# The loads of split q and k with the head dimension as outermost index

## What is computed

```python
# B = 16, N = 512, D = 128, H = 16 heads, hd = 8
qkv = x @ w_qkv + b_qkv
q, k, v = jnp.split(qkv, 3, axis=-1)             # each to (B, H, N, hd)
q = jax.nn.elu(q) + 1
k = jax.nn.elu(k) + 1
attn_num = jnp.einsum('bhid,bhjd->bhij', apply_rope(q), apply_rope(k))
attn_denom = jnp.einsum('bhid,bhjd->bhij', q, k)
out = jnp.einsum('bhij,bhjd->bhid', attn_num / attn_denom, v)
x = x + out.transpose(0, 2, 1, 3).reshape(B, N, D) @ w_out + b_out
```

## Time and profile before

| | us |
|---|---|
| median of 3 runs | 4204.29 (4202.71 to 4212.35) |
| the profiled execution, its own time | 4196.47 |
| its span, from the first to the last instruction | 4194.5 |
| PE busy | 3514.4 (84%) |
| ACT busy | 3228.1 (77%) |
| DVE busy | 2902.8 (69%) |
| POOL busy | 1500.8 (36%) |

### The profile page before, as it was taken

The page is one execution under the profiler, slowest core; times in us unless marked ns, Lnnn a source line. Parts: engine busy times, 40 slices in busy tenths (PEclk is TensorE's granted clock), DMA queues, the critical chain, the costliest instruction groups (busy, mean ns, idle before and its releaser), DMA issues.

```text
span 4194.5 us, 39166 instructions
## 1 busy us (share of the span) xinstructions
PE 3514.4 (84%) x11446; PEld 1492.4 (36%) x11446; DVE 2902.8 (69%) x3513; ACT 3228.1 (77%) x4037; POOL 1500.8 (36%) x758
## 2 busy tenths in 40 slices
PE   3877598988889898988889898898989888898857
PEld 1131243433333343333334333333334333333423
DVE  2426568768686767868686777858677786858592
ACT  2667588887888787888878888888878888786653
POOL 1112244435243443524344342524434252414361
PEclk9586699999999999999999999999999999998977
DMA  3131244444444444444443444434444444434432
GB/s 120 37 120 58 96 127 147 134 140 129 133 135 126 137 140 130 132 130 136 129 143 122 144 130 131 137 124 141 129 138 133 132 139 133 129 109 135 133 122 86
DMA packets 184390, 526.88 MB, mean 126 GB/s; under 512 B 19217, under 2 KB 66162, under 8 KB 184178
## 3 DMA queue, kind: packets, MB, share of 16 engines
q1 hardware_dynamic: 184178, 524.38, 39.5%
HBM read 488.65 MB, written 38.01 MB: 126 GB/s over the span
## 4 chain that ended last, share of the span: by engine, by line
PE 42%; DVE 16%; ACT 13%; issue 11%; DMA 10%; SPq 7%; POOL 1%; ACTq 0%; POOLq 0%; DVEq 0%
PE bank L782 13%; DMA bc<-bcscr 6%; PE bank L771 4%; PE bank L673 4%; PE bank L734 4%; ACT L1022 4%; ACT rPool L884 3%; SPq L583 3%; DMA kpk<-kscr 3%; PE bank L773 3%; PE bank L712 3%; PE bank L772 3%; DVE ws L1220 3%; SPq L584 3%; PE bank L707 3%
## 5 line engine op out<-in xcount | busy, mean ns | idle before, releaser
L782 PE MATMUL bank<-hF,wst 128*128 128x512 f32 x2304 | 1200.8, 637 | 39.5 <-DVE tmp L1178 34.0
L884 ACT ACTIVATE hF<-bank,cols 128x512 f32<-128x512 f32 x1152 | 770.6, 686 | 362.4 <-PE bank L773 352.7
L1108 DVE TENSOR_TENSOR rPool<-bank,rPool 128x512 f32<-128x512 f32 x1024 | 699.7, 683 | 500.6 <-PE bank L712 470.5
L1313 POOL TENSOR_TENSOR acc<-acc,tmp 128x512 f32<-128x512 f32 x240 | 428.0, 1783 | 1300.3 <-DVE tmp L1178 1297.7
L1328 POOL TENSOR_TENSOR yM<-yM,ws 128x1024 f32<-128x1024 f32 x240 | 699.7, 2915 | 485.1 <-DVE ws L1227 474.4
L884 ACT ACTIVATE rPool<-bank 128x512 f32<-128x512 f32 x1040 | 573.9, 594 | 254.4 <-PE bank L707 202.8
L771 PE MATMUL bank<-xnH,wst 128*128 128x512 f32 x1152 | 648.3, 563 | 90.0 <-ACT hF L884 69.0
L1022 ACT ACT_TABLE_LOAD x531 | 681.3, 1283 | 9.4
L1220 DVE TENSOR_TENSOR_SCAN ws<-dAs,ws 128x1024 f32<-128x1024 f32 x256 | 674.9, 2636 | 5.9 <-ACT dAs L884 3.4
L712 PE MATMUL bank<-qpk,kpk 48*128 48x512 bf16 x1024 | 424.4, 414 | 257.0 <-DVE rPool L1108 255.7
L782 PEld LDWEIGHTS bank<-hF,wst 128*128 128x128 f32 x2304 | 423.3, 199 | 466.1 <-issue 365.3
(11 more groups left out here) (154 smaller groups left out, 3064.2 us busy)
## 6 DMA issues: line engine op xcount, KB each, us to landing
wst<-wscr SPq DMA_DIRECT2D x288, 768.0 KB, 5.9
bc<-bcscr SPq DMA_DIRECT2D x256, 512.0 KB, 4.1
cB<-gscr SPq DMA_DIRECT2D x256, 256.0 KB, 4.8
qscr<-parts SPq DMA_DIRECT2D x32, 384.0 KB, 9.6
kscr<-parts SPq DMA_DIRECT2D x32, 384.0 KB, 3.0
kpk<-kscr SPq DMA_DIRECT2D x128, 96.0 KB
qpk<-qscr SPq DMA_DIRECT2D x128, 96.0 KB
kpk<-kscr SPq DMA_DIRECT2D x128, 64.0 KB
```

The lines of the kernel that those rows point to most:

```text
L782: pe.matmul(ps[FFN][:, :], w2, hF[:, q % HSLOTS, :], start=(c == 0), stop=(c == FC - 1)).then_inc(s_dn, 1)
L884: return nc.scalar.activation(out_, in_, fn, **kw)
L1108: v.tensor_tensor(rP[:, step % 2, c, :], ps[NUM][:, :], rP[:, step % 2, c, :], ALU.mult).then_inc(s_mul, 1)
```

## The change

Both DRAM views get the order "d a (c t)" in place of "a d (c t)": the head dimension (8) becomes the outermost index of each load's source, the part (3, 2 or 1) the second. The destination slices are the same, so partition r * 8 + d * many + a now holds what partition r * 8 + a * 8 + d held. This is so for q and for k, so that each product in the 48-row sum keeps its partner and only its place moves. No instruction is added or removed.

```diff
                 for u in range(2):
-                    qs = qscr[b, u, :, heads, :].rearrange("a (d c) t -> a d (c t)", c=NC)
-                    ks = kscr[b, u, :, heads, :].rearrange("a (d c) t -> a d (c t)", c=NC)
+                    qs = qscr[b, u, :, heads, :].rearrange("a (d c) t -> d a (c t)", c=NC)
+                    ks = kscr[b, u, :, heads, :].rearrange("a (d c) t -> d a (c t)", c=NC)
                     for r, part, many in ((0, 0, 3), (3, 1, 2), (5, 2, 1)):
                         here = slice(HALF * u + HD * r, HALF * u + HD * (r + many))
-                        sp.dma_start(kpk[here, k % 2, :], ks[0:many]).then_inc(s_k_ld[k % 2], 16)
-                        sp.dma_start(qpk[here, k % 2, :], qs[part:part + 1].broadcast_to([many, HD, NC * 512])).then_inc(s_q_ld[k % 2], 16)
+                        sp.dma_start(kpk[here, k % 2, :], ks[:, 0:many]).then_inc(s_k_ld[k % 2], 16)
+                        sp.dma_start(qpk[here, k % 2, :], qs[:, part:part + 1].broadcast_to([HD, many, NC * 512])).then_inc(s_q_ld[k % 2], 16)
```

## The result

The changed kernel takes 4032.15 us (median of 4 runs, 4031.18 to 4033.69) against 4203.5 us (4196.35 to 4212.35) for the kernel before in the same comparison. The ratio is 0.9592 with a 95% interval of 0.9573 to 0.961: 4.1% faster, 171 us. In the profiled executions the span goes from 4194.5 to 4029.4 us, 165.1 less.

The account below looks back on a forecast made before the run. No engine is full; slow head loads back up a few DMA engines, stopping the core. Waits 115 + start 20 + clock 15 = 150 us, five sixths kept, 125: 4204 to about 4080 us, range 4025 to 4168.

Parts of the forecast that it names:

- The cause: Loads of heads: 3.7 busy engines at 74 GB/s need 10.6 us against 7.4 of issuing; the next DMA queues behind.
- The issue time: SP's queue: the 12 DMAs of a load keep their issue time, about 7.4 us a load; no change taken.
- B: SP's queue: issue time grows moderately, 4.3 us more a load; gain only 60 us, 4145 us; chance 0.11.
- E: SP's queue: issue time grows in proportion to the outer count, 10.2 us more a load; slower, 4329 us; chance 0.07.
- A: SP's queue: issue of the eight larger DMAs falls to 0.3 us; gain 172 us, 4030 us; chance 0.10.
- The waits: Steady passes: PE's 31.3 us for kpk and DVE's 83.8 us for bc all go, 115 us.
- the start: Three double loads before the passes: the pieces behind them shorten by about 6 + 5 + 9 = 20 us.
- the clock: Behind each pass's stop: 4.5 us at half speed cost 2.2 us, 29 over 13 passes; half counted, 15.
- five sixths: Cut on the whole 150 us ceiling for remaining PE-DVE waits and ACT's fixed order; 125 us kept.
- the uncut sum: Steady passes: 115 us of waits plus the clock's full 29 us, before halving the clock and before the final cut.
- The clock's dips: Sign in the profile: the drops of the clock once a pass are gone.
- C: Passes: only the kpk wait goes and bc stays late by other traffic; gain 41 us, 4163 us; chance 0.05.

Follow-up runs that it names:

- bcfirst_before: Kernel before, slow loads kept, SP's order changed so the bc load behind each ahead load stands in front of it: 4131.83 us, ratio 0.9833.
- the isolated loads: Changed kernel plus seven loads behind its last output, three times over, each waited for: 3 x 8 took 3.91 us with issue, 8 x 3 2.71.
- only2: Kernel before with the new index order only in the 64 KB DMAs (32 KB ones unaffected by order): 4057.74 us, ratio 0.9654.
- only3: Kernel before with the new index order only in the 96 KB DMAs (32 KB ones unaffected by order): 4043.97 us, ratio 0.9618.
- issue2: Changed kernel with each of a load's 12 DMAs cut in two halves of its columns, 24 DMAs, same bytes: 4187.96 us, ratio 0.9954.
- six: Changed kernel with six scratch slots of parts, so a load needs four DMAs, not 12: 4020.98 us (0.9571) in three rounds, 4023.57 (0.9569) in five.

## Why the prediction was right, and where its size was off

**The cause.** Slow loads hold a few DMA engines, and what is issued behind them waits there: right, by `bcfirst_before` (the place in the queue), by the isolated loads (the order of the indices, 2.0 us against 0.6), and by `only2` and `only3` (no proportion to the changed bytes). That the outermost index of 8 would let a load keep up with its issuing, 106 GB/s, held: 120 GB/s move at a share of 0.40.

**The issue time.** Kept, as I took it: 0.68, 0.66, 0.65, 0.65 against 0.72, 0.70, 0.63, 0.62; 6 of the 768 issues took more than 1 us. B and E, which let it grow with the outer count, fall. A let it shrink to 0.3 us, and falls too: alone, 8 x 3 was issued in 0.66 us where flat rows took 0.32. A's 4030 lies nearest to the measured 4032, but its mechanism did not happen; the agreement is luck.

**The waits.** All 115 us of them are gone from the steady passes. The first load of the passes starts at 548.29 us before and at 524.81 after, so the start gave 23.5 us; I had 20. The last `kpk` DMA is at 3725.2 and 3557.3 us, 167.9 earlier, so the passes gave 144.4, and 3 were given back at the end. These are the passes in one window each, before and after (columns as in the earlier trace rows):

```profile
548.29:3725.20 3176.91, 2807.87 (x9399) 1201.65 (x9391) 2337.71 (x2817) 2635.67 (x3306) 1227.21 (x615) 0.96 0.43 133
524.81:3557.30 3032.49, 2750.05 (x9398) 1173.59 (x9391) 2369.91 (x2817) 2634.69 (x3306) 1285.56 (x615) 0.97 0.45 140
```

PE stood idle 369.0 us of them before and 282.4 after. So of the 144.4 us PE's idle time gave 86.6, and 57.8 came from its busy time, with the same matmuls. Over the whole run the two are 111.8 and 53.3. The idle time fell by less than the 115 us of waits. Its own waits for `kpk` fell by 46 us over the run, and those for DVE at L712, which stood behind the waiting L1216, by 74; they were, in the kernel before:

```profile
PE bank L712 <- DVE rPool L1108: 255.7, 220, 9.2
```

Against that, PE's wait for DVE at L782 grew by 27 us (34.0 to 61.4). DVE's busy time grew too, by 32 us with the same instructions: the mean of L1220 went from 2636 to 2721 ns, that of L1227 from 1592 to 1676. Why these take longer no run shows.

**The mis-sized term is the clock.** I took one dip a pass of about 4.5 us, 29 us in all, counted half of it, and then kept five sixths of everything. For the waits that last cut was not too hard: 86.6 is three quarters of 115. But the clock gave back far more than 15. Summed over the trace's clock records, the passes held 283 us at half clock (1.2 GHz) before and 160 after, and PE was busy in 255 and 159 us of them. Half of these 96 us, 48 us, is what the clock gave back in the passes, an estimate that takes the work at half clock to last twice as long. Over the whole run PE was busy at half clock for 518 us before and 412 after; half of the difference, 53 us, is the whole fall of its busy time. A pass before had three to five dips, not one; two of them, of 6.8 to 10.2 and 3.4 to 6.8 us, stand behind the two late `bc` loads. That the uncut sum, 115 + 29 = 144, equals the measured 144.4 is luck: PE's idle time gave 28 us less than the 115, and its busy time 29 more than the 29. `issue2` shows the link between waits and clock from the other side: there the waits come back without the slow loads, and with them 40 us of PE's busy time (3501.5) and the lower clock (0.919).

**The clock's dips** are not gone, as I had said they would be. Each pass after the change still has one of 6.8 us behind the first ahead load (the clock is 0.89 over 2014 to 2026 us) and one of 3.4 us behind the second, which was up to 6.8:

```profile
2063.90 4.54 PE L782 MATMUL bank<-hF,wst 128*128 128x512 f32 x6 [2.18 <-DVE tmp L1178]
```
```profile
2064.00:2068.00 4.00, 4.00 (x6) 1.55 (x6) 4.00 (x3) 1.08 (x3) 3.86 (x3) 0.57 0.94 272
```

PE had stood 2.18 us for DVE just before, in the wait at L782 that grew.

**C** said that only the `kpk` waits would go. It falls: of the 94.8 us of waits for `bc` 7.0 are left.

## What to carry to other kernels

Look at the outermost index of the source of each DMA. Here 3 or 2 left a transfer on two to three of 16 engines, and most of the price (84 of 115 us in the passes) was paid by the next DMA in the queue, not by the slow one. Compare a transfer's time with its issuing. Once it was the shorter here, fewer DMAs still gave 12 us (`six`), and twice as many took the gain away. When a stop of all engines goes, look for two things beside its length: the waits that grow in its place, and the slow clock behind it, of which the trace can give the sum.

## What the runs showed of the hardware

- The issue of a DMA mostly took 0.60 to 0.84 us where the source had two indices of rows and the destination one run of partitions, in either order of the two. It took 0.28 to 0.33 in the isolated loads of flat rows. Halving the bytes changed nothing (0.64). The smallest DMAs of the kernel, with a part index of 1, took 0.43 to 0.53 us for k and about 0.3 for q; why these differ is open.
- Alone, 96 KB in 24 rows moved in 2.0 us with 3 as the outermost count and in 0.6 us with 8.
- A load on few engines delayed a load to 128 partitions issued behind it from about 4 us to 11.75 us, though more than three quarters of the DMA engines' time was free while it was issued (share 0.23).
- Twelve small issues in a row were 7.4 us of SP's time, and 12 more cost this kernel 156 us (4032 to 4188), although SP's waits for other engines sum to 3075 us of 4029 in the changed kernel.
- After the change TensorE still ran at half clock for some us in each pass; in the pass shown, one such stretch (0.57 over 2064 to 2068 us) followed a wait of only 2.18 us.
